# A two-layer decoder on four interleaved chains: grouped head sums, scores turned by key parity, small work moved from VectorE to GpSimd, a bias folded, setup reordered, and new step lists

## What is computed

```python
x = x + local_attention(norm(x))        # "a": 16 heads, window of 7 taps, softmax over taps, mixed with a fixed table
x = x + masked_cross_attention(norm(x), ctx, mask)   # "b": keys and values are ctx itself
x = x + slot_mixer(norm(x))             # "f": top 8 of 64 slots, a GRU step on the slots, out @ wo.T + bo
x = x + causal_attention(norm(x))       # "1": with a learned position bias
x = x + cross_attention(norm(x), ctx)   # "x"
x = x + quantized_mlp(norm(x))          # "g": ternary weights, depthwise conv of 3, silu
# local_attention, per head:   scores[l, w] = sum_d Q[l, d] * K[l + w - 3, d] / 4,   w = 0..6
# weight_quant(w) = clip(round(w / mean(|w|)), -1, 1) * mean(|w|)
# slot_mixer: out = alpha @ (S_new @ wv.T + bv); return out @ wo.T + bo
```

## Time and profile before

| | us |
|---|---|
| median of 3 executions | 3631.13 |
| lowest, highest | 3620.27, 3642.56 |
| the profiled execution | 3635.76 |
| its span, first to last instruction | 3633.8 |
| PE busy | 3113.3 (86% of the span) |
| DVE busy | 2590.4 (71%) |
| ACT busy | 2178.2 (60%) |
| POOL busy | 555.5 (15%) |
| TensorE clock granted, mean | 0.943 of full |

### The profile page before, as it was taken

One profiled execution on the slowest core, in us unless ns is written; L12 is line 12 of the kernel. 1 busy time (PEld: TensorE's weight loads), 2 busy tenths in 40 slices (PEclk: granted clock), 3 DMA queues, 4 the chain that ended last, 5 costly groups with the idle time before them and its releaser, 6 DMA issues.

```text
span 3633.8 us, 64290 instructions
## 1 busy us (share of the span) xinstructions
PE 3113.3 (86%) x25516; PEld 2222.2 (61%) x25516; DVE 2590.4 (71%) x5788; ACT 2178.2 (60%) x4268; POOL 555.5 (15%) x1040
## 2 busy tenths in 40 slices
PE   2589987899889998899888998899988998879995
PEld 1446764577556666567665666566655676656663
DVE  4575678765896568875888667866788657886667
ACT  1236863477645775566755676557764577646773
POOL 0231002210121101211022101211012110122000
PEclk9789998999989999999999999889999999989996
DMA  3000000000000000000000000000000000000000
GB/s 130 30 1 1 1 14 21 8 1 4 11 21 9 1 4 21 11 8 1 14 19 11 1 4 11 21 8 1 11 14 11 8 1 14 11 11 8 1 4 9
DMA packets 45965, 45.28 MB, mean 12 GB/s; under 512 B 11120, under 2 KB 43632, under 8 KB 45536
## 3 DMA queue, kind: packets, MB, share of 16 engines
q1 hardware_dynamic: 45664, 41.17, 3.8%
HBM read 32.77 MB, written 8.39 MB: 11 GB/s over the span
## 4 chain that ended last, share of the span: by engine, by line
PE 61%; DVE 19%; ACT 11%; issue 4%; DMA 3%; POOL 2%; SPq 1%; DVEq 0%; POOLq 0%; ACTq 0%
PE banks L1172 9%; PE banks L1203 9%; PE banks L1249 6%; PE banks L1311 5%; PE banks L1212 4%; PE banks L1245 3%; PE banks L1332 3%; DVE chain_m L670 2%; PE banks L1275 2%; PE banks L1188 2%; PE banks L1290 2%; DVE chain_arena L747 2%; DVE chain_arena L875 2%; ACT chain_arena L1006 2%; PE banks L1390 2%
## 5 line engine op out<-in xcount | busy, mean ns | idle before, releaser
L670 DVE TENSOR_REDUCE chain_m<-banks 128x4 f32<-128x512 f32 x512 | 332.6, 684 | 192.4 <-PE banks L1203 191.3
L1203 PE MATMUL banks<-chain_arena 64*128 64x256 f32 x3072 | 448.2, 415 | 24.5 <-DVE chain_m L670 12.2
L1203 PEld LDWEIGHTS banks<-chain_arena 64*128 64x128 f32 x3072 | 280.6, 194 | 155.3 <-issue 93.8
L1027 ACT ACTIVATE chain_arena<-chain_arena,chain_m 128x128 f32<-128x128 f32 x1024 | 323.8, 395 | 77.9 <-DVE chain_m L670 77.2
L1500 POOL TENSOR_TENSOR chain_rs<-chain_rv,neg_half 128x2 f32<-128x2 f32 x192 | 147.5, 768 | 1360.6 <-DVE chain_ng L655 1359.7
L1249 PEld LDWEIGHTS banks<-chain_arena 64*128 64x128 f32 x4096 | 256.8, 193 | 113.3 <-issue 113.3
L1249 PE MATMUL banks<-chain_arena 64*128 64x128 f32 x4096 | 306.9, 291 | 0.0
L961 ACT ACTIVATE chain_xn<-chain_xa,chain_nm,chain_rs 128x256 f32<-128x256 f32 x384 | 209.5, 596 | 152.4 <-POOL chain_nm L1503 151.4
L668 DVE TENSOR_TENSOR chain_arena<-banks,pos_bias 128x512 f32<-128x512 f32 x256 | 175.2, 684 | 149.7 <-PE banks L1203 149.3
L1212 PE MATMUL banks<-chain_arena,chain_va 128*32 128x128 f32 x5120 | 194.2, 278 | 34.1 <-ACT chain_arena L1006 21.3
L1006 ACT ACTIVATE chain_arena<-banks,chain_mask_k 128x1024 f32<-128x1024 f32 x128 | 142.9, 1117 | 109.5 <-PE banks L1249 109.0
(11 more groups left out here) (310 smaller groups left out, 6968.3 us busy)
## 6 DMA issues: line engine op xcount, KB each, us to landing
...
```

What stands on the lines that cost most here:

```text
L670: e.tensor_reduce(t["m"][:, b, r, :], t["s"][:, u % 4] if bias else bank(c, u % 2), AX.X, ALU.max, negate=True).then_inc(*done(f"{tag}_mx{ ...
L1027: ex = e.activation(s, s, ACT.Exp, bias=t["m"][:, u // GROUPS, row_group(u), a:a + 1])
L1203: mm[i] = e.matmul(c.ps[:, i, 2 * T * j:2 * T * j + 2 * T], t["qh"][p, j, x, b, :], flat(t["kx"][p, j, b]), start=not masked, stop=not mas ...
```

## The change

1. **Head sums of four taps at once.** `window_tensor` has two steps in place of seven: taps 0 to 3, then 4 to 6, with j outside and the taps inside. The step waits for all its products.
2. **Turned scores by key parity.** A unit is now one sequence and one parity o of the key heads; the two query halves stand side by side, so four matmuls of 64x128 by 64x256 replace eight by 64x128. The maxima are stored in another order (`maxima_vector`, `max_of`), and `heads_tensor` picks its parts by a function. The split's tiles are read in plain order.
3. **From DVE to GpSimd.** `ng` of each norm, `va` and the bf16 mask, and the additions `a_ac3` and `a_ac5`; in the ring the products 5 and 6 wait for GpSimd's additions.
4. **Slot bias folded.** `bof` is added to `bvo` once in setup, and L1411 goes.
5. **Setup.** SP loads in another order, ACT issues 19 of the loads before its own work, and the MLP weights are treated ahead of `pos_eps`.
6. **Lists.** All strings of `ORDER` are new, SP has one of its own (the context DMA is a step apart from the rest), and every engine starts with chain 3, where it started with chain 0.

```diff
+    "sync": (
+        "0011223330310212303102123300112233001122330011223300112233001122"),
     "pool": (
-        "0120312301230101200121330122233013201323010210023113220003311001220021101122132320321330332132301302"
...
+        "3012330011223012333300300301201112223001231201320132012303013320012331133220000333330300011130022120211"
...
@@ -261,13 +260 @@
...
+    e.dma_start(k["cpar"][:], rows(inp["c_param"])).then_inc(ld["cpar"], 16)
+    e.dma_start(k["lmul"][:], rows(inp["l_mult"])).then_inc(ld["lmul"], 16)
...
@@ -296,0 +289,14 @@
+    for name in ("wihT", "wqkvxT", "woxT"):
+        e.dma_start(k[name][:], tiles(inp[name])).then_inc(ld[name], 16)
+
+
+def loads_scalar(e, k, inp, ld):
+    for name in ("ident", "parity", "third", "rows_of", "half", "expand", "head_sum"):
+        e.dma_start(k[name][:], inp[name]).then_inc(ld[name], 16)
+    for name, blocks in (("w1t", KT), ("w2t", HT)):
+        e.dma_start(k["f_" + name][:].rearrange("p (k n) -> p k n", k=blocks), tiles(inp[name])).then_inc(ld["f_" + name], 16)
+    for name in ("wvf", "wofT"):
+        e.dma_start(k[name][:], tiles(inp[name])).then_inc(ld[name], 16)
+    for name in ("wproj", "w1bT", "wqkv0T", "wo0T", "wpT", "w1aT", "wqkv1"):
+        e.dma_start(k[name][:], tiles(inp[name])).then_inc(ld[name], 16)
+    e.dma_start(k["w2fT"][:], inp["w2fT"]).then_inc(ld["w2fT"], 16)
@@ -336,0 +343,16 @@
+
+    for name, bank in (("w1t", 6), ("w2t", 7)):
+        w, a = k["f_" + name], k["a_" + name]
+        e.wait_ge(ld["f_" + name], 16)
+        e.tensor_reduce(a[:], w[:], AX.X, ALU.add, apply_absolute_value=True).then_inc(*done(name + "_abs"))
+        e.wait_ge(*pe(name))
+        e.tensor_scalar(k[name + "_mean"][:], ps[:, bank, 0:1], 1.0 / (HID * D), 1e-5, ALU.mult, ALU.max).then_inc(*done(name + "_mean"))
+        e.wait_ge(*dve(name + "_mean"))
+        e.tensor_scalar(k[name + "_back"][:], k[name + "_mean"][:], 1.0 / 127 if name == "w1t" else 0.5 / 127, None, ALU.mult)
+        e.reciprocal(a[:], k[name + "_mean"][:]).then_inc(*done(name + "_rec"))
+        e.wait_ge(*dve(name + "_rec"))
+        e.tensor_scalar(w[:], w[:], a[:, 0:1], ROUND, ALU.mult, ALU.add).then_inc(*done(name + "_round"))
+        e.wait_ge(*dve(name + "_round"))
+        e.tensor_scalar(w[:], w[:], -ROUND, 1.0, ALU.add, ALU.min).then_inc(*done(name + "_min"))
+        e.wait_ge(*dve(name + "_min"))
+        e.tensor_scalar(k[name][:], w[:], -1.0, None, ALU.max).then_inc(*done(name))
@@ -443 +465,2 @@
-    e.tensor_copy(k["bvo"][:], ps[:, 7, 0:D]).then_inc(*done("bvo"))
+    e.wait_ge(ld["bof_r"], 16)
+    e.tensor_tensor(k["bvo"][:], ps[:, 7, 0:D], k["bof_r"][:], ALU.add).then_inc(*done("bvo"))
@@ -449,16 +471,0 @@
-    for name, bank in (("w1t", 6), ("w2t", 7)):
...
@@ -495,0 +503,3 @@
+    for name, bank in (("w1t", 6), ("w2t", 7)):
+        e.wait_ge(*dve(name + "_abs"))
+        e.matmul(ps[:, bank, 0:1], k["ones"][:], k["a_" + name][:], start=True, stop=True).then_inc(*done(name))
@@ -526,0 +537 @@
+    e.wait_ge(*dve("w2t_mean"))
@@ -629,0 +637,7 @@
+def max_of(m, b, r, a):
+
+    i = 2 * (a // 2) + r % 2
+    j = 2 * (r // 2) + a % 2
+    return m[:, b, i, j:j + 1]
+
+
@@ -655 +668,0 @@
-    e.tensor_scalar(t["ng"][:], t["sv"][:, :, 0], -1.0, None, ALU.mult).then_inc(*done(f"{tag}_ng"))
@@ -670,2 +683,3 @@
-        e.tensor_reduce(t["m"][:, b, r, :], t["s"][:, u % 4] if bias else bank(c, u % 2), AX.X, ALU.max,
-                        negate=True).then_inc(*done(f"{tag}_mx{u}"))
+        s = t["s"][:, u % 4] if bias else bank(c, u % 2)
+        m = t["m"][:, b].rearrange("p (j x) (i o) -> p x i j o", x=2, o=2)[:, u // 2 % 2, u % 2]
+        e.tensor_reduce(m, s.rearrange("p (j o) t -> p j o t", o=2), AX.X, ALU.max, negate=True).then_inc(*done(f"{tag}_mx{u}"))
@@ -703,2 +717,2 @@
-        if w >= RING:
-            e.wait_ge(*pe(f"a_sc{w - RING}"))
+        if w == RING:
+            e.wait_ge(*pe("a_sc0"))
@@ -749,4 +762,0 @@
-    def add(name, slot, other, after):
-        e.wait_ge(*dve(after))
-        e.tensor_tensor(flat(ring[:, slot]), flat(ring[:, slot]), flat(ring[:, other]), ALU.add).then_inc(*done(name))
-
@@ -757,14 +767,6 @@
-    add("a_ac3", 2, 3, "a_pv3")
-    yield
-    e.wait_ge(*pool("a_ac1"))
-    weighted(4, 1)
-    yield
-    e.wait_ge(*dve("a_ac3"))
-    weighted(5, 3)
-    yield
-    add("a_ac5", 2, 3, "a_pv5")
-    yield
-    e.wait_ge(*dve("a_ac5"))
-    weighted(6, 3)
-    yield
-    add("a_ac6", 2, 3, "a_pv6")
+    for w, slot, free in ((4, 1, "a_ac1"), (5, 3, "a_ac3"), (6, 1, "a_ac4")):
+        e.wait_ge(*pool(free))
+        weighted(w, slot)
+        yield
+    e.wait_ge(*dve("a_pv6"))
+    e.tensor_tensor(flat(ring[:, 0]), flat(ring[:, 0]), flat(ring[:, 1]), ALU.add).then_inc(*done("a_ac6"))
@@ -772 +774 @@
-    e.wait_ge(*pool("a_ac4"))
+    e.wait_ge(*pool("a_ac5"))
@@ -926,8 +927,0 @@
-
-    e.wait_ge(c.ctx, 16 * (n + 1))
-    e.wait_ge(c.mask_c, 16 * (n + 1))
-    e.tensor_tensor(by_head(t["va"][:]), t["xn"][:].rearrange("p b (h c) -> p b h c", c=DH),
-                    spread(spread(t["mask_c"][:], 2, H), 3, DH), ALU.mult).then_inc(*done("c_va"))
-    e.wait_ge(c.mask_r, 16 * (n + 1))
-    e.tensor_scalar(t["mask_bf"][:], t["mask_r"], 0.0, -MASKED, ALU.is_equal, ALU.mult).then_inc(*done("c_mask"))
-    yield
@@ -1059 +1053 @@
-    e.wait_ge(*pe("a_sc6"))
+    e.wait_ge(*pe("a_sc1"))
@@ -1212 +1206 @@
-        mm = e.matmul(out[32 * a:32 * a + 32, :], c.t["va"][:, b, VH * h:VH * h + 32], p[:, a, :], start=True, stop=True)
+        mm = e.matmul(out[32 * a:32 * a + 32, :], c.t["va"][:, b, VH * h:VH * h + 32], p(a), start=True, stop=True)
@@ -1221 +1215 @@
-        e.wait_ge(*dve("c_mask"))
+        e.wait_ge(*pool("c_mask"))
@@ -1239 +1233 @@
-        b, x = u // 2, u % 2
+        b, o = u // 2, u % 2
@@ -1243 +1237 @@
-            e.wait_ge(*act(f"{tag}_ex{u - 1}" if x else f"{tag}_ou{b - 1}"))
+            e.wait_ge(*act(f"{tag}_ex{u - 1}" if o else f"{tag}_ou{b - 1}"))
@@ -1245,2 +1239,2 @@
-            e.matmul(ps[:, i, :], k["pick"][:, 2 * i + x, :], flat(t["mT"][:, b]), start=True, stop=False)
-        for a in range(PER):
+            e.matmul(ps[:, i, :], k["pick"][:, 2 * i + o, :], flat(t["mT"][:, b]), start=True, stop=False)
+        for j in range(KT):
@@ -1249,2 +1243,2 @@
-                mm = e.matmul(ps[:, i, T * a:T * a + T], t["kx"][p, a // 2, b, a % 2, :], t["qh"][p, a // 2, x, b, :], start=False,
-                              stop=a == PER - 1)
+                mm = e.matmul(ps[:, i, 2 * T * j:2 * T * j + 2 * T], t["kx"][p, j, b, o, :], t["qh"][p, j, :, b, :], start=False,
+                              stop=j == KT - 1)
@@ -1253 +1247 @@
-        if x:
+        if o:
@@ -1256 +1250 @@
-                mm = heads_tensor(e, c, b, r, ps[:, 0, T * r:T * r + T], t["p"][:, r % 2, r // 2])
+                mm = heads_tensor(e, c, b, r, ps[:, 0, T * r:T * r + T], lambda a: t["p"][:, a % 2, r // 2, 2 * (a // 2) + r % 2, :])
@@ -1328,3 +1322,4 @@
-    for w in range(WIN):
-        e.wait_ge(*pool("a_qk3") if w == 3 else dve(f"a_qk{w}"))
-        r = 32 * (w % 4)
+    for i, last in enumerate(("a_qk2", "a_qk6")):
+        e.wait_ge(*dve(last))
+        if i == 0:
+            e.wait_ge(*pool("a_qk3"))
@@ -1332,3 +1327,5 @@
-            mm = e.matmul(ps[r:r + 32, 1, N * (w // 4):N * (w // 4) + N], k["head_sum"][:, 32 * j:32 * j + 32],
-                          flat(t["ring"][:, w % RING, j]), start=(j == 0), stop=(j == KT - 1))
-        mm.then_inc(*done(f"a_sc{w}"))
+            for w in range(RING * i, min(RING * i + RING, WIN)):
+                r = 32 * (w % RING)
+                mm = e.matmul(ps[r:r + 32, 1, N * i:N * i + N], k["head_sum"][:, 32 * j:32 * j + 32],
+                              flat(t["ring"][:, w % RING, j]), start=(j == 0), stop=(j == KT - 1))
+        mm.then_inc(*done(f"a_sc{i}"))
@@ -1411,2 +1408 @@
-        e.matmul(ps[:, b, 0:D], k["pick"][:, 1, :], k["bias3"][:], start=True, stop=False)
-        mm = e.matmul(ps[:, b, 0:D], t["alT"][p, :], t["sval"][p, :], start=False, stop=True)
+        mm = e.matmul(ps[:, b, 0:D], t["alT"][p, :], t["sval"][p, :], start=True, stop=True)
@@ -1498,0 +1495,2 @@
+    e.wait_ge(*dve(f"{tag}_mv1"))
+    e.tensor_scalar(t["ng"][:], t["sv"][:, :, 0], -1.0, None, ALU.mult).then_inc(*done(f"{tag}_ng"))
@@ -1501 +1498,0 @@
-    e.wait_ge(*dve(f"{tag}_ng"))
@@ -1511 +1508 @@
-    m3 = t["m3"][:].rearrange("p b a r s -> p b r a s")
+    m3 = t["m3"][:]
@@ -1533,0 +1531,7 @@
+
+    e.wait_ge(c.ctx, 16 * (n + 1))
+    e.tensor_tensor(by_head(t["va"][:]), t["xn"][:].rearrange("p b (h c) -> p b h c", c=DH),
+                    spread(spread(t["mask_c"][:], 2, H), 3, DH), ALU.mult).then_inc(*done("c_va"))
+    e.wait_ge(c.mask_r, 16 * (n + 1))
+    e.tensor_scalar(t["mask_bf"][:], t["mask_r"], 0.0, -MASKED, ALU.is_equal, ALU.mult).then_inc(*done("c_mask"))
+    yield
@@ -1540,5 +1544,5 @@
-    for w, after in ((1, "a_pv1"), (4, "a_pv4")):
-        e.wait_ge(*dve(after))
```

(13 more changed lines are left out.)

294 lines of the change are left out of this document (134 added, 160 removed).

## The result

The changed kernel takes 3399.3 us (median of 4 runs, 3397.0 to 3404.6) against 3632.3 of the kernel before on the same chip: a ratio of 0.936, 95% interval 0.933 to 0.939. That is 233 us less. The forecast was 102 less, and its range ended at 3430.

The account below looks back on a forecast made before the run. PE was taken as the bound, but not alone. From 3633.8 us, setup and start took 21 and PE work 81, DVE/POOL and lists 0; adjusted for span and profiled run, 3529 us, range 3430 to 3625.

Parts of the forecast that it names:

- I take 0: New engine lists: worth nothing, as chain spacing looked alike; range 90 us either way, a quarter of PE's 362 us idle.
- the clock only as a danger: Rival for PE's clock: less work with the same waits doubles low-clock stretches, 157 us lost, 3686 us; chance 0.07.
- Its own sign: Timeline check: if PE's busy time falls by 80 us and the span by much more, the lists did it.
- The first rival: New lists also gather a quarter of PE's 362 us idle time: 90 us more, 3440 us; chance 0.25.
- Passing through whole: All 81 us of PE work saved shorten the span, rather than 57 us, as DVE gets looser too.
- The chain's quotient: PE's chain share over its busy share, 61 over 86: 0.7 to 1 us back per us of PE work removed.
- Head sums, 40: PE's head sums: each piece costs 1.0 us whatever is in it, pieces go from 103 to 63, 40 us less.
- Turned scores, 8: PE's turned scores: 256 groups go from 1.09 to 1.06 us each, 8 us less.
- Slot bias, 33: Slot mixer on PE: without biases two mixtures overlap in 0.63 us, 1.04 less over 32 turns, 33 us.
- DVE and POOL, net 0: Moves to GpSimd: DVE loses 111 us (worth 30), POOL gains 197 (costs 26); they cancel, ends 60 us either side.
- Setup, -21: Setup and start: 26 us gained by load order and earlier MLP weights, 5 lost at the start; between -10 and -30.
- Half of PE's saving lost to latencies: Rival: half of PE's saving goes to other chains' latencies, POOL's additions cost 5 us more; 3575 us, chance 0.14.

Follow-up runs that it names:

- setup_alone: The kernel before with only the new setup (load order, loads split between SP and ACT, MLP weights quantised first): 3604.9 us.
- replanned_old: setup_alone with its old operations kept and single list steps moved wherever an event model came out shorter: 3512.8 us.
- replanned_from_old: All new operations and the new setup, under lists made from those of before by moving single steps with an event model: 3438.0 us.
- joined_alone: setup_alone plus only the joined head sums, four taps in one step and three in another, products and additions as before: 3611.8 us.
- old_operations: The changed kernel's lists and setup with the operations of the kernel before, missing steps placed where their data come: 3708.4 us.
- replanned_new: The changed kernel with only its lists changed, single steps moved wherever an event model came out shorter: 3349.1 us.
- fold_alone: setup_alone plus only the slot bias folded into bvo, lists unchanged: 3587.3 us.

## Why the prediction was wrong

**Lists: "I take 0" is the step that failed.** The forecast missed 130 us. Under the old lists the new operations made it no faster (3613 against 3605), and moving list steps alone gave 92. Going from before over setup_alone, replanned_old and replanned_from_old to the changed kernel, setup has 27 us, the lists 92, the operations in fitted lists 75, and the lists once more 39: 131 us for the lists in all. The forecast had compared how evenly the chains' turns start and how long the pieces are. Neither tells whether a step stands where its data come. That places decide is shown by replanned_old, where only places changed; what a bad place does was looked at only in joined_alone, where the joined step holds PE and then DVE.

**Half clock.** The forecast priced all work at the high level and had the clock only as a danger. It gave 59 us of the 234. Its own sign, PE's busy time lower by 80 us, missed this too: busy time fell by 173, as time at the low level counts as busy. Over the runs the clock's loss goes with the idle time: 178 and 612 us in old_operations (about 597 without the missing records), 148 and 521 before, 96 and 429 in replanned_old, 69 and 410 in replanned_new. From end to end that is 109 for 187, so with a microsecond of idle time about 0.6 of clock came or went. Single runs lie some 10 us off such a line: fold_alone has 6 us more idle time than its base and 15 more of clock.

**The first rival** had the mechanism, at 90 us and a chance of 0.25. It was wrong in calling a quarter of the idle time the most that lists could gather, and it left the clock out. Its evidence against, "the lists before look just as well spaced", was the same mistaken test.

**Passing through whole.** "The whole of PE's 81 us passes through": under the old lists 0.55 of the fold's came through and nothing of the head sums'; in the new lists 0.76 of the fold's; and 0.59 to 0.76 of all in fitted lists. The chain's quotient, 0.71, was nearer.

**Head sums, 40.** Work went from 115.7 to 62.9 us, 53. After, 1.0 us for each piece holds. Before, the 103 pieces of the list cost 1.1 each, as waits cut some of them: four pieces with a wait inside took 2.7 to 4.5 us of work. The sum of PE's work was 98, not 81; most of what is left over is this. What the joined head sums are worth in the new lists was not tried by itself.

**Turned scores, 8.** 279.3 to 271.0 us of work. **Slot bias, 33:** 52.5 to 20.3. Both right as work.

**DVE and POOL, net 0.** POOL's 752 us were right (750). Under the old lists, the only ones in which the moves were tried alone, net 0 doesn't hold: +32 us. What they are worth in the new ones was not tried by itself. DVE lost 51 us and not 111; see the last section.

**Setup, -21.** The term was 26 for setup and 5 back at the start. The memsets went from 119.94 to 97.58, 22 instead of 26, and `rel_norm` from 50.52 to 43.45 us, 7 instead of 11.6: DVE began on the MLP weights at 27.86 us and not near 19, so they lasted to 42.2 us and were not wholly hidden. The two runs on setup give 27, within their uncertainty of 22. The 5 us at the start came: the first projection is 16.8 us earlier.

**The other rivals.** Half of PE's saving lost to latencies, and GpSimd's additions in the way: both are seen under the old lists (3613), and neither makes the time in the new. The clock didn't fall. The Trainium skill, "TensorEngine Tiling (Array Packing)", Theoretical Speedup, read as a rule for the edit, gave 3409. The time came out near it by chance: head sums gave 53 us of work and not 160.
